# A mixture-of-experts stage turned round: weights stationary and 256 tokens moving, with the products of x apart from those of the mask

## The reference, cut to what matters

```
scores = softmax(x @ gate_w.T)                       # 64 experts
topk_w, topk_idx = top_k(scores, 8)
w_e   = zeros(N, 64).at[..., topk_idx].add(topk_w)
flat  = w_e[:, inv_map]                              # 8 groups of 8
scalar = flat.sum(-1)                                # a share per token and group
soft  = softmax(where(flat == 0, NEG_INF, flat), -1)
xg = x[:, None, :] + einsum('ngi,ghi->ngh', soft, mask_up_w)
g = einsum('ngh,gih->ngi', xg, gate_proj_w)          # i: 176 per group
u = einsum('ngh,gih->ngi', xg, up_proj_w)
a = silu(g) * u
d = einsum('ngi,ghi->ngh', a, down_proj_w)
y = einsum('ng,ngh->nh', scalar, d)
```

## Time and profile before

| | us |
|---|---|
| median of three runs | 234.39 (234.38 to 235.89) |
| span of the profiled execution | 233.6 |
| the profiled execution's own time (span and what lies around it, taken as the median) | 234.4 |
| granted TensorE clock, mean | 0.998 |

### The profile page before, as it was taken

How to read it: one execution, slowest core, us unless ns; L and a number is a source line. 1 busy time by engine, 2 the same in 40 slices (tenths; PEclk the granted TensorE clock), 3 DMA queues, 4 the chain that set the end, 5 groups by cost and what they waited for, 6 DMA issues and landing times.

```text
span 233.6 us, 4695 instructions
## 1 busy us (share of the span) xinstructions
PE 222.1 (95%) x1600; PEld 214.4 (92%) x1600; DVE 176.0 (75%) x494; ACT 111.2 (48%) x231; POOL 83.6 (36%) x143
## 2 busy tenths in 40 slices
PE   6899789989999999999999999999999999999994
PEld 5899787879999999999999999999999999988883
DVE  4277979998999999789977697743777566555874
ACT  2233257932444450654364464748724772335443
POOL 4569997656647631100503433002022102010520
PEclk9999999999999999999999999999999999999999
DMA  6699864000000001500000000000000100010011
GB/s 181 164 356 222 260 210 130 1 0 3 0 1 3 0 3 22 203 4 0 0 3 0 0 3 1 4 0 0 3 0 0 39 9 3 0 46 0 4 46 45
DMA packets 14055, 11.51 MB, mean 49 GB/s; under 512 B 2928, under 2 KB 13776, under 8 KB 14032
## 3 DMA queue, kind: packets, MB, share of 16 engines
q1 hardware_dynamic: 13936, 11.16, 15.9%
q10 hardware_dynamic: 96, 0.05, 0.1%
HBM read 10.14 MB, written 1.07 MB: 48 GB/s over the span
## 4 chain that ended last, share of the span: by engine, by line
PE 75%; DVE 7%; SPq 6%; DMA 6%; issue 2%; ACT 2%; POOL 1%; ACTq 0%; DVEq 0%; POOLq 0%
PE bank L758 26%; PE bank L596 14%; PE bank L603 11%; PE bank L761 4%; PE bank L829 4%; DMA ring<-in_up_p 4%; PE bank L813 3%; PE bank L647 2%; PE bank L649 2%; PE bank L648 2%; PE bank L799 1%; SPq L552 1%; SPq L561 1%; PE bank L787 1%; DMA lags<-in_kernel_rev 1%
## 5 line engine op out<-in xcount | busy, mean ns | idle before, releaser
L758 PE MATMUL bank<-w_split,xt 128*128 128x352 f32 x384 | 69.0, 328 | 0.2 <-issue 0.2
L758 PEld LDWEIGHTS bank<-w_split,xt 128*128 128x128 f32 x384 | 61.0, 188 | 0.4 <-issue 0.4
L1256 DVE SCALAR_TENSOR_TENSOR act<-silu,scal,bank 128x176 f32<-128x176 f32 x64 | 22.6, 393 | 19.2 <-ACT silu L961 19.0
L596 PE MATMUL bank<-d_split,a_t 128*128 128x256 f32 x264 | 33.4, 285 | 0.0
L596 PEld LDWEIGHTS bank<-d_split,a_t 128*128 128x128 f32 x264 | 32.2, 192 | 0.0
L961 ACT ACTIVATE silu<-bank 128x352 f32<-128x352 f32 x32 | 14.9, 465 | 33.5 <-PE bank L761 33.4
L1414 POOL TENSOR_TENSOR fold<-prod 128x256 f32<-128x256 f32 x32 | 23.7, 742 | 9.7 <-DVE att L1113 6.5
L1403 POOL TENSOR_TENSOR kv<-ctx_ext 128x640 f32<-128x640 f32 x16 | 20.0, 1254 | 6.5 <-PE bank L649 3.9
L838 ACT ACTIVATE a_t<-bank 128x384 fp32r<-128x384 f32 (+1 forms) x32 | 14.8, 461 | 13.5 <-PE bank L603 13.4
L1354 POOL TENSOR_SCALAR ve<-mv 128x2 f32<-128x2 f32 (+2 forms) x11 | 3.0, 276 | 44.9 <-DVE mv L1049 44.9
L1016 DVE TENSOR_TENSOR a_t<-bank,a_t 128x384 fp32r<-128x384 f32 (+1 forms) x32 | 16.6, 518 | 2.8 <-ACT a_t L838 2.8
(11 more groups left out here) (151 smaller groups left out, 451.8 us busy)
## 6 DMA issues: line engine op xcount, KB each, us to landing
toe<-lag_rows SPq DMA_DIRECT2D x4, 512.0 KB, 7.7
ring<-in_down_p SPq DMA_DIRECT2D x2, 704.0 KB, 4.6
ctx<-in_ctx_rows SPq DMA_DIRECT2D x2, 512.0 KB, 5.0
ring<-in_gate_p SPq DMA_DIRECT2D x2, 512.0 KB, 6.8
ring<-in_up_p SPq DMA_DIRECT2D x2, 512.0 KB, 8.8
out_x<-x_res SPq DMA_DIRECT2D x3, 256.0 KB, 2.1
tern_w<-in_w_fc SPq DMA_DIRECT2D x1, 640.0 KB, 4.3
tern_w<-in_w_proj SPq DMA_DIRECT2D x1, 640.0 KB, 5.5
```

Source lines behind the costliest of these rows:

```text
L596: last = pe.matmul(dst, lhs(a), rhs(b), start=start and i == 0, stop=stop and i == 2)
L758: pe.matmul(psum((name, b, c))[:, 0:CW], lhs, w_split[:, w, kt, part, cols], start=i == 0, stop=False)
L1256: drain(dve.scalar_tensor_tensor(out=act[:, g * NI:(g + 1) * NI], in0=silu[:, n % 2, cols], scalar=scal[:, b, g:g + 1], in1=psum(("up", b, ...
```

## The change

1. **x products and mask products are steps of their own.** The unit of work is now a group `g` of two batches (256 tokens) and a pair `c` of tiles of 128 of the 1408 columns (six pairs, the last of one tile). `xpart` has 24 products per pair with the weights stationary (`w_split`) and `xt` moving, 256 columns; `mpart` adds the mask products (`m_stack` stationary, `soft_t` moving) later. The result is transposed already: act lies as tiles of 128 hidden columns by 256 tokens.
2. **No transposes of act.** `turn_a` is gone. The tile that straddles the two mask halves takes its mask rows from a new small matrix `m_cut`, which POOL clears at the start and ACT fills by four copies.
3. **The share lies along the columns now.** A new step `share` makes 8 rows of 256 tokens from `top_t` and `members` (the one-hot matrix summed by group, one more DVE instruction), ACT copies them, SP stores them to DRAM (`share_rows`), and 18 loads per group spread them over partitions into three slots (`share`), at most three pairs ahead. The DVE reduction into `scal` is gone.
4. **The product in two parts.** DVE multiplies up bank and share into `act`, POOL multiplies `act` with silu (new on POOL), ACT copies the upper part (`act_hi`), DVE makes the lower part (`act_lo`).
5. **down** goes pair by pair, both batches of the group in one bank, `act_hi`/`act_lo` stationary, `d_split` moving; one DVE update of `x_res` for both batches.
6. **Order and banks.** `TIMES` is new throughout, bank choice as well (three banks instead of two in the middle, seven at the end). SP follows `SCHEDULE` too, behind the ring loads.

```diff
-    "weights": [-4492, -4480, -2066, -2061, -1755, -1687, -1214, -1195, -1096, -839, -794, -638, -627, -618, -618,
-        -567, -486, -486, -257, -162, -82, 29, 186, 323, 323, 327, 449],
+    "weights": [22, 25, 26, 27, 37, 38, 54, 55, 58, 61, 62, 63, 64, 65, 70, 79, 81, 91, 92, 98, 101, 114, 115, 119,
+        130, 131, 132],
...
+def pieces_of(r):
+
+    lo, hi = r * P, (r + 1) * P
+    cuts = [lo] + [k for k in range(0, GI, NI) if lo < k < hi] + [hi]
+    return [(a // NI, a - lo, b - lo) for a, b in zip(cuts, cuts[1:])]
...
+            def share_load(n):
+
+                g, c = divmod(n, PAIRS)
+                if c == 0:
+                    sp.wait_ge(share_stored[g], 16)
+                if n >= SLOTS:
+                    wait_drained(sp, ("up",) + divmod(n - SLOTS, PAIRS))
+                for t, r in enumerate(tiles_of(c)):
+                    for k, p0, p1 in pieces_of(r):
+                        src = bass.AP(share_rows.tensor, (g * NG + k) * NT, [[0, p1 - p0], [1, NT]])
+                        sp.dma_start(share[p0:p1, n % SLOTS, t, :], src).then_inc(share_loaded[n % SLOTS], 16)
...
+                elif kind == "share":
+                    r = step[1]
+                    pe.wait_ge(members_made, 1)
+                    claim(pe, step)
+                    fill(pe.matmul(psum(step)[0:NG, 0:NT], members[:, :], top_t[r][:, :], start=True, stop=True), step)
+                elif kind == "xpart":
...
                     for w, name in enumerate(("gate", "up")):
+                        claim(pe, (name, g, c))
+                        for part in range(2):
+                            if c == 0 and w == 0:
+                                wait_drained(pe, ("turn_x", g), part + 1)
+                            for t, r in enumerate(tiles_of(c)):
+                                for kt in range(2):
+                                    for wp in range(2 - part):
+                                        pe.matmul(psum((name, g, c))[:, t * NT:(t + 1) * NT],
+                                                  w_split[:, w, kt, wp, r * P:(r + 1) * P], xt[half][:, kt, part, cols],
+                                                  start=part + t + kt + wp == 0, stop=False)
...
-                elif kind == "turn_a":
-                    _, b, c = step
-                    wait_drained(pe, ("up", b, c))
-                    turn(step, [(act[:, r * P:(r + 1) * P], P, P) for r in DONE_TILES[c]])
                 elif kind == "down":
...
+                    pe.wait_ge(act_low, n + 1)
+                    for t, r in enumerate(tiles_of(c)):
+                        for k in range(RQ):
+                            rows = slice(k * P, (k + 1) * P)
+                            both = (act_hi[:, n % 2, t, rows], act_lo[:, n % SLOTS, t, rows])
+                            for i, (pa, pd) in enumerate(((0, 0), (1, 0), (0, 1))):
+                                last = pe.matmul(psum(("down", g))[:, k * L:(k + 1) * L], both[pa], d_split[:, r, pd, :],
+                                                 start=r + k + i == 0, stop=r == TILES - 1 and k == RQ - 1 and i == 2)
+                    last.then_inc(down_done, 1)
...
+                    if n >= SLOTS:
+                        dve.wait_ge(down_done, n - SLOTS + 1)
+                    dve.wait_ge(share_loaded[n % SLOTS], 16 * loads_before(n))
+                    wait_filled(dve, ("up", g, c))
+                    flat = [t[:, n % SLOTS].rearrange("p t n -> p (t n)")[:, 0:w] for t in (act, share)]
+                    drain(dve.tensor_tensor(flat[0], psum(("up", g, c))[:, 0:w], flat[1], ALU.mult), ("up", g, c))
...
+                    wait_drained(pool, ("gate", g, c))
+                    wait_drained(pool, ("up", g, c))
+                    a = act[:, n % SLOTS].rearrange("p t n -> p (t n)")[:, 0:w]
+                    pool.tensor_tensor(a, a, silu[:, n % 2].rearrange("p t n -> p (t n)")[:, 0:w],
+                                       ALU.mult).then_inc(act_made, 1)
```

More of the change, by code:

```diff
@@ L166, in check_order @@
     at = {step: i for i, step in enumerate(schedule)}
-    for r in range(RUNITS):
-        for b in range(r * RQ, (r + 1) * RQ):
-            assert at["flat", r] < at["chunk", b, 0]
-    for b in range(B):
-        for c in range(NCH):
-            assert at["chunk", b, c] < at["turn_a", b, c]
-        assert at["turn_a", b, NCH - 1] < at["down", b]
+    for g in range(RUNITS):
+        assert at["turn_x", g] < at["xpart", g, 0] and at["turn_soft", g] < at["mpart", g, 0]
+        assert at["flat", g] < at["share", g] < at["mpart", g, 0]
+        for c in range(PAIRS):
+            assert at["xpart", g, c] < at["mpart", g, c] < at["act", g, c] < at["down", g, c]
     for u, bs in enumerate(UNITS):
-        assert at["down", bs[-1]] < at["stat", "cross", u]
+        assert at["down", bs[-1] // RQ, PAIRS - 1] < at["stat", "cross", u]
         if u:
@@ L184, in check_order @@
     assert at["consts",] < at["turn_att", 0, 0] and at["onehot",] < at["turn_top", 0]
-    assert at["mask",] < at["scores", 0]
+    assert at["mask",] < at["scores", 0] and at["mask",] < at["tern_abs", "fc"] and at["onehot",] < at["share", 0]
+    assert at["turn_down", 5] < at["mpart", 0, 0]
+    assert at["share", 0] < at["turn_fc", 0] and at["share", 1] < at["turn_proj", 0]
+    assert at["share", 3] < at["hidden", 0, 0]
     for w in ("gate", "up"):
@@ L208, in plan_psum @@
     early = [G0, U0, G1, U1, TR]
[L209 to L211 removed]
+    mixed = [Y0, Y1, TR]
+    last = [G0, U0, G1, U1, TR, Y0, Y1]
+    n_early = n_mixed = n_last = 0
     uses, n_use, n_read = {}, [0] * 8, [0] * 8
[L213 removed]
+    first_chunk = SCHEDULE.index(("xpart", 0, 0))
     conv_end = SCHEDULE.index(("gather", 1, HEADS // 2 - 1))
[L215 removed]
+    tail = SCHEDULE.index(("mpart", RUNITS - 1, PAIRS - 1))
     conv = 0
@@ L223, in free_one, with use @@
         return n
-    def use(key, bank, reads):
+    def use(key, bank, reads, fills=1):
         uses[key] = (bank, n_use[bank], n_read[bank], reads)
-        n_use[bank] += 1
+        n_use[bank] += fills
         n_read[bank] += reads
     reads = {"turn_ctx": 2, "turn_q": 2, "turn_router": 2, "turn_w": 2, "mask_up": 1, "turn_down": 2, "tern_sum": 1,
-             "turn_fc": 1, "turn_proj": 1, "turn_att": 1, "turn_x": 2, "logits": 1, "turn_top": 1, "flat": 3,
-             "turn_soft": 1, "turn_0": 1, "turn_1": 2, "scores": 1, "turn_p": 1, "read": 1, "hidden": 1, "out": 1}
+             "turn_fc": 1, "turn_proj": 1, "turn_att": 1, "turn_x": 2, "logits": 1, "turn_top": 1, "flat": 2,
+             "share": 1, "keep": 0, "turn_soft": 1, "turn_0": 1, "turn_1": 2, "scores": 1, "turn_p": 1, "read": 1, "hidden": 1, "out": 1}
     by_batch = ("scores", "read", "out")
@@ L499, in updates_of_x @@
         elif which == "cross":
-            for b in batches_of(which, k):
-                wait_drained(eng, ("down", b))
+            for g in sorted({b // RQ for b in batches_of(which, k)}):
+                wait_drained(eng, ("down", g))
         else:
```

286 lines of the change are left out of this document (167 added, 119 removed), and 49 rows, old and new, of the table TIMES.

## The result

The changed kernel takes 240.78 us (median of 4 runs, 240.16 to 241.45) against 234.39 us: ratio 1.0245, 95% interval 1.0209 to 1.0281 (the quotient of the two medians alone is 1.027). It is 2.4% slower, where 1.9% faster was forecast. Its profiled execution took 240.56 us, with a span of 238.8.

The account below looks back on a forecast made before the run. PE's instruction stream was taken as the bound, plus about 20 us of ramp, waits and tail. -4.7 - 0.7 - 0.3 + 0.3 + 1.0 = -4.4 us, from 234.4 to 230.0 us; range 227.0 to 235.5.

Parts of the forecast that it names:

- What bounds the kernel before: Whole kernel: time is PE's instruction stream plus about 20 us of ramp, short waits and tail.
- The stream, -4.7: PE's products: transposes removed -9.7, x products +2.0, mask products +1.3, share +1.7, down 0; sum -4.7 us.
- Waits that go, -0.7: PE's waits for act at its removed transposes: the largest 0.45 us, shorter ones put at 0.25; -0.7 us.
- The front, -0.3: Up to turn_x of group 0: PE restarts at 30.12, reaches turn_x at 50.9 with more work ahead; -0.3 us.
- Cost 0: Chain from mask product to down product: 3.5 us, covered on PE by 5.0, 3.4 or 6 to 19 us.
- None of the three becomes the bound: DVE, ACT and POOL loads: DVE's part about 39 to 31 us, ACT about even, POOL gains 25; none bounds.
- DVE's backlog: Rival: DVE, 93% busy from 48 to 63 us, runs late; 3.4 us go back, 233.4 us; chance 0.17.
- First pair's gate bank, +0.3: First pair's gate bank: 0.9 us of cover against silu 0.6 plus a table load of 1.28; +0.3 us.
- Share through DRAM: Share rows stored and loaded: 7.3 and 8.9 us, hidden behind 10.3 us of PE's order, 14 to 16 later.
- that rival: Share comes late: SP issues of 1.68 us make DVE wait for share; 238.5 us, from 0.77 per issue; chance 0.14.
- The tail, +1.0: After the last down: batches 6 and 7 come free together, less cover between steps; +1.0 us (0 to +2.5).
- the signs listed: Right: 0.120 spacing, first x product 62 to 63 us, PE over 99% busy; wrong: act_lo waits, x product after 64.

Follow-up runs that it names:

- e10_twice: Kernel before the change with each of its 88 turn_a transposes issued twice; ratio 1.0465 to the kernel before, 10.9 us more.
- e2_mask: Changed kernel with the mask step (two VectorE mask operations, two ternary loads on SyncE) moved earlier in the order; ratio 1.0147 to the kernel before.
- e9_nopool: Changed kernel without GpSimd's product by silu, ScalarE's act copy waiting for VectorE's mask product instead; ratio 0.9986 to the kernel before.
- e11_order: Changed kernel with its whole table of order numbers laid anew, every instruction the same, order and banks different; ratio 0.9946 to the kernel before.
- e8_more: Changed kernel with the first x product of each gate and up bank issued twice (48 products more); ratio 1.0318 to the kernel before.
- e1: Changed kernel with one convolution (conv 0,10) moved ahead of the keep step and the up weights' first transposes; ratio 1.0219 to the kernel before.

## Why the prediction was wrong

- **What bounds the kernel before: right.** e10_twice shows PE's stream at full price.
- **The stream, -4.7: right.** 0.120 us per product of 256 columns with a weight stationary, 4.8 us less in all (4.4 with the share products as measured). The gap that the Trainium skill ("TensorE: Matmul & The Clock Gate", section "Back-to-back issue gap") gives for 256 columns by its rule, 109 ns, is not what these products show: 0.120. The section itself calls this the gap of an isolated product, too low for few columns where weights are loaded in between; the prediction took it for the rule of a stream.
- **Waits that go, -0.7: wrong in effect.** In their place came 2.3 us of idle time for act_lo and 1.5 for silu.
- **The front, -0.3: wrong by 1.6 us.** "PE restarts at 30.12 again" held (30.27). But "fewer products stand ahead of the landing, so the wait there grows as the other shrinks" counted the idle time only. turn_x 0 came at 52.5, not 50.9: the clock at its half cost 1.6. It was not in the sum, and in some executions it isn't there: PE restarted at 30.67 in e2_mask's, without a fall, and reached turn_x 0 at 51.24.
- **"Cost 0" for the chain from mask product to down: this is the main step that failed.** In its place stand the 2.3 us for act_lo. The chain's length was about right (GpSimd's product of 512 columns takes 1.34 us, not 1.1), and PE's cover was counted from the order. But the cover was counted as PE's time alone. VectorE stands in the chain twice, in order, and waits in it for GpSimd and ScalarE (12.0 us); what its queue holds behind comes late, at down 0,5 the mask step and tern_abs, and PE pays at a step that isn't the chain's neighbour. "Behind DVE's wait stand convolution products" was written down and given no price. e9_nopool and e11_order each halve that wait, and both end PE's waits for act_lo; that the wait's length, and not its place, does it is not shown (e8_more has all of it and nearly no wait of PE).
- **"None of the three becomes the bound", and no term for VectorE ahead of the first x product: the second step that failed.** From 48 to 63 us VectorE is busy for 14.1 of 15 us (14.0 before, when PE didn't wait for it), and PE is idle for it three times between turn_x 0 and 64.3 us, 1.9 us in all, before any mask product is made. The prediction counted this stretch by PE's work alone. In all ten runs with this order the three waits are the same, in e9_nopool too, so they don't come from GpSimd's product; which move of the order brought them is not tested.
- **DVE's backlog, as a rival, was the right mechanism at a third of its size.** 233.4 us stood for 3.4 us given back; the waits between turn_x 0 and the last down grew by 7.1. The argument against it (VectorE has 5 us less to do) took busy time for readiness: over the middle VectorE is idle for 38 us and still late. It also counted VectorE's instructions at their undisturbed lengths, while they took 8.0 us more beside GpSimd's passes.
- **First pair's gate bank, +0.3:** 0.87 us of PE idle, since the table load began only when the mask product was there (75.65), not behind the copy that ended at 74.34.
- **Share through DRAM: hidden, as forecast**; 6 issues took 4.05 us, 0.68 each, under the 0.77 from which that rival decides. What was missed is that they stand ahead of the ternary loads on SyncE: 1 us at down 0,5. That rival's 238.5 us is the recorded number nearest to the result, by chance: its mechanism, VectorE waiting for share, isn't in the trace.
- **The tail, +1.0: 1.6**, of the forecast kind (0.53 us for qt, 1.14 for pt, 0.96 for hid_t). In e11_order it is 2.4; why, no run shows.
- Of the signs listed, "PE waiting for act_lo in the middle" and "a first x product after 64 us" (65.62) came true. Of the signs of being right, only the spacing of 0.120 held: PE was busy for 97% of the middle and not 99, an SP issue took 0.68 us and not 0.5, a DMA ended 0.94 us of VectorE's idle time, and from the last down to the end it took 26.2 us and not 21 to 23.

## What to carry to other kernels

When a change puts a longer chain across in-order engines, count what each engine in it waits for as well as the bound engine's cover: an engine that is busy for three quarters of a stretch can be late for work that has nothing to do with the chain. Count the same for the stretch before the chain begins. A form and its order are timed together; the same instructions here took 1.0245 and 0.9946 of the time before. To see whether a kernel is bound by one engine's stream, give it more of it: 9.7 us of transposes cost 10.9 us in one kernel, 5.8 us of products cost 1.7 (3.5 in the trace) in the other.

## What the runs showed of the hardware

- PE's granted clock fell to its half for 3.4 us at about 30 us in some executions and not in others, after idle times of 2.1 to 2.8 us with a fall and 1.8 to 3.3 us without one, in kernels whose program up to there is the same but for one convolution (e1). In it the records of the convolutions stood 0.27 us apart instead of 0.136, and 1.6 us were lost.
- An ACT_TABLE_LOAD (1.28 us) was not issued ahead of the wait of the instruction that needs it: at 75.65 it began when PE's product was there, with ScalarE idle for 1.31 us before it.
- VectorE instructions that read no PSUM bank took up to 0.94 us longer while GpSimd was in a pass: xn of 256 columns took 1.24 to 1.34 us in four cases instead of 0.40, of which two stood beside `kv` products and two beside the new product. VectorE instructions that read a bank didn't show it.
- GpSimd's product of two fp32 operands, 512 columns, takes 1.34 us, 2.0 times VectorE's 0.68 for the like.
- The up weights' landing scatters: over the seven kernels with the changed kernel's front, PE had waited between 10.2 and 11.7 us up to its restart there, and 9.0 and 7.8 us in the two with e11_order's, so that one profile of this kernel is uncertain by more than 1 us.
